# Graph attention on images: the output stores move from SyncE's DMA queue to ScalarE's, one slot later

## The reference, cut to what matters

```
alpha = relu(bn(wa @ x));  sigma = relu(bn(ws @ x))          # 32 x 2048 each
att   = softmax(mask8(alpha.T @ sigma))                       # each pixel sees its 8 neighbours
h_s   = x @ att.T
catt  = softmax(mask_pm1(x @ x.T))                            # each channel sees its two neighbours
h_p   = catt @ x
out   = (1 - gama) * x + gama * elu(h_s + h_p)
```

## Time and profile before

| | |
|---|---|
| Time, median of 3 runs | 399.77 us (397.32 to 403.58) |
| Profiled execution | 396.9 us, of which its span is 395.1 us |
| Busy PE, DVE, ACT, POOL | 355.2, 315.1, 306.2, 291.6 us |
| Granted TensorE clock, mean | 0.972 |
| DMA queue of SP | 136.76 MB |
| DMA queue of ACT | 0.07 MB |

### The profile page before, as it was taken

How to read it: one execution, slowest core, us unless ns; L and a number is a source line. 1 busy time by engine, 2 the same in 40 slices (tenths; PEclk the granted TensorE clock), 3 DMA queues, 4 the chain that set the end, 5 groups by cost and what they waited for, 6 DMA issues and landing times.

```text
span 395.1 us, 14345 instructions
## 1 busy us (share of the span) xinstructions
PE 355.2 (90%) x5487; PEld 270.0 (68%) x5488; DVE 315.1 (80%) x1072; ACT 306.2 (77%) x900; POOL 291.6 (74%) x198
## 2 busy tenths in 40 slices
PE   4869999999999999998999999899999999999663
PEld 1437868676786868677686768678676868768553
DVE  1065978889798878979897887979888897988894
ACT  3166788897878798887879788787878888787881
POOL 2103788878887888788778977887888778878980
PEclk8779999999999999999999999999999999999995
DMA  7999999999999999999999999999999999995124
GB/s 243 413 362 395 371 372 375 363 383 359 398 384 375 381 365 365 372 393 374 371 410 374 380 347 402 368 395 372 376 394 360 387 358 396 360 316 210 74 92 159
DMA packets 40613, 137.74 MB, mean 349 GB/s; under 512 B 3296, under 2 KB 3552, under 8 KB 36448
## 3 DMA queue, kind: packets, MB, share of 16 engines
q1 hardware_dynamic: 40256, 136.76, 92.8%
q10 hardware_dynamic: 288, 0.07, 0.1%
HBM read 103.26 MB, written 33.55 MB: 346 GB/s over the span
## 4 chain that ended last, share of the span: by engine, by line
PE 53%; DVE 23%; ACT 12%; issue 8%; DMA 2%; SPq 0%; DVEq 0%; ACTq 0%
PE z L468 22%; PE gb L468 21%; PE tr L543 7%; ACT score L281 7%; DVE probs L374 6%; DVE elu L389 5%; ACT z L301 3%; DVE z L383 3%; PE score L468 3%; DMA x<-x_dram 2%; DVE gb L404 2%; DVE band L400 1%; DVE row_inv L370 1%; ACT elu L308 1%; ACT probs_t L292 1%
## 5 line engine op out<-in xcount | busy, mean ns | idle before, releaser
L468 PEld LDWEIGHTS z<-probs_t,upper 64*128 64x128 f32 x2304 | 153.6, 189 | 44.6 <-issue 29.7
L468 PE MATMUL z<-probs_t,upper 64*128 64x128 f32 (+1 forms) x2304 | 171.3, 282 | 4.7 <-ACT probs_t L292 2.1
L247 POOL TENSOR_TENSOR blend<-elu,blend 128x1024 f32<-128x1024 f32 x62 | 146.2, 2358 | 9.5 <-POOL elu L243 0.4
L243 POOL TENSOR_SCALAR elu<-elu,vec,mix 128x1024 f32<-128x1024 f32 x62 | 74.0, 1193 | 76.4 <-DVE elu L389 76.3
L389 DVE SCALAR_TENSOR_TENSOR elu<-elu,z 128x512 f32<-128x512 f32 x124 | 79.5, 683 | 27.5 <-ACT elu L308 27.0
L308 ACT ACTIVATE elu<-z 128x512 f32<-128x512 f32 x128 | 69.7, 597 | 39.4 <-PE z L468 39.4
L301 ACT ACTIVATE z<-x,catt 128x512 f32<-128x512 f32 x128 | 83.6, 693 | 14.1 <-DVE catt L421 13.9
L383 DVE SCALAR_TENSOR_TENSOR z<-near,catt,z 128x512 f32<-128x512 f32 x128 | 90.4, 753 | 1.5 <-ACT z L301 1.5
L281 ACT ACTIVATE score<-score,neg_max 128x128 f32<-128x128 f32 x256 | 86.2, 337 | 6.2 <-DVE neg_max L365 6.2
L237 POOL TENSOR_SCALAR blend<-x,mix 128x1024 f32<-128x1024 f32 x64 | 72.0, 1125 | 7.4 <-DMA x<-x_dram 7.4
L468 PE MATMUL gb<-x,wt 128*32 128x256 f32 (+2 forms) x720 | 65.9, 484 | 2.1 <-DMA x<-x_dram 2.1
(11 more groups left out here) (49 smaller groups left out, 142.7 us busy)
## 6 DMA issues: line engine op xcount, KB each, us to landing
x<-x_dram SPq DMA_DIRECT2D x32, 1024.0 KB, 8.4
near<-x_near_dram SPq DMA_DIRECT2D x64, 512.0 KB, 7.7
out_dram<-blend SPq DMA_DIRECT2D x62, 512.0 KB, 7.0
upper<-x_t_dram SPq DMA_DIRECT2D x16, 1152.0 KB, 8.9
upper<-x_t_dram SPq DMA_DIRECT2D x16, 1024.0 KB, 9.0
out_dram<-blend SPq DMA_DIRECT2D x4, 256.0 KB, 2.0
const<-constants_dram SPq DMA_DIRECT2D x1, 291.5 KB, 12.8
const<-constants_dram SPq DMA_DIRECT2D x1, 128.0 KB, 2.2
```

Source lines behind the costliest of these rows:

```text
L243: nc.gpsimd.tensor_scalar(elu[s % 2][:, :, :], elu[s % 2][:, :, :], vec[:, V_GAMA:V_GAMA + 1], mix[:, 1:2], ALU.mult, ALU.add).then_inc(ga ...
L247: nc.gpsimd.tensor_tensor(blend[s % BLENDS][:, :, :], elu[s % 2][:, :, :], blend[s % BLENDS][:, :, :], ALU.add).then_inc(blend_done, 1)
L468: return nc.tensor.matmul(o, l, r, start=start, stop=stop, skip_group_check=True, **kw)
```

## The change

SP no longer stores. ACT does, on its own queue: at the beginning of slot t it waits for the blend of step t-3 and asks for its store, before `move_odd`, `move_even` and `exp_z` of that slot. Step 63 is stored after the loop. The waits, sizes and semaphores of each store stay as they were.

```diff
@@ SP's program
-            def store(s):
-                b, q = s // QUARTERS, s % QUARTERS
-                if s < TAIL:
-                    sp.wait_ge(blend_done, s + 1)
-                    sp.dma_start(out_img[b, :, :, q * QN:(q + 1) * QN], blend[s % BLENDS][:, :, :])\
-                        .then_inc(stored[s % BLENDS], 16)
...
                 if b + 1 < B:
                     load_near(b + 1, q)
-                if real(t - 2):
-                    store(t - 2)
@@ ACT's program
+            def store(s):
+                b, q = s // QUARTERS, s % QUARTERS
+                if s < TAIL:
+                    act.wait_ge(blend_done, s + 1)
+                    act.dma_start(out_img[b, :, :, q * QN:(q + 1) * QN], blend[s % BLENDS][:, :, :])\
+                        .then_inc(stored[s % BLENDS], 16)
+                else:
+                    for h in range(HALF):
+                        act.wait_ge(tail_done, 2 * (s - TAIL) + h + 1)
+                        act.dma_start(out_img[b, :, h, q * QN:(q + 1) * QN], blend[s % BLENDS][:, h, :])\
+                            .then_inc(stored[s % BLENDS], 16)
...
             for t in range(STEPS + 2):
                 b, q = t // QUARTERS, t % QUARTERS
                 ahead = b + 1 < B
+                if real(t - 3):
+                    store(t - 3)
                 if q == 1 and ahead:
                     move_odd(b + 1)
...
                 if q == 1 and ahead:
                     move_query(b + 1)
+            store(STEPS - 1)
```

## The result

The changed kernel takes 463.68 us in the median of 4 runs (460.32 to 466.3), the kernel before 398.54; the ratio is 1.169, with a 95% interval of 1.163 to 1.175. The profiled execution took 466.3 us, its span is 464.5.

The account below looks back on a forecast made before the run. PE was taken to bound the kernel before. 62 turns of 6.40 us plus moves of 6.3 and 7.7 give 410.8 against 349.6: +61.2 on a span of 395.1, 456.3; with run allowances 459 us, range 453 to 469.

Parts of the forecast that it names:

- the sum: From `exp_z` of step 0 to that of step 62: 62 turns plus the moves, 410.8 us against 349.6 before.
- The wait at the head closes a loop through POOL.: `exp_z`, DVE's elu, two POOL operations, ACT's store, next `exp_z`: one turn per slot, 5.75 us up to the issue.
- The issue costs 0.57 + 0.08 us.: On ACT after the wait: 0.57 us issue plus 0.08 to the next activation, making a plain turn 6.40 us.
- The first rival: On ACT: the issue doesn't hold ACT, only the wait does; a turn of 5.83, 424 us; chance 0.10 with cases between.
- The moves cost 0.45 and 0.51.: On ACT between store and `exp_z`: `move_odd` adds 0.45 us in 14 slots, `move_even` 0.51 in 15.
- The delay of DVE at q = 0 costs nothing.: DVE's elu, late behind the channel softmax in slots q = 0, costs nothing; at most 4.4 us.
- SP's relief and the landing cost nothing.: SP losing 62 + 4 store issues gains nothing; store landings, covered by two slots, cost nothing.
- "81% is more than that": PE, 81% busy after the change, keeps clock 1.00, since 68% busy between 375 and 385 had clock 1.00.
- The rival: Slower still: PE's gaps let the granted clock fall; over half of the images 34 us more, 493 us; chance 0.11.
- The DMA engines aren't a hidden bound.: Despite a DMA share of 1.02, DMA doesn't pace the kernel before: it has only 2% of the chain.
- What the profile after should show.: Turns 6.3 to 6.5 or about 6.9 us, ACTq rows 0.53 to 0.63, ACT idle over 1, DMA share near 0.87.
- A slot takes about 5.67 us because PE needs that.: In the kernel before, PE is busy 21.55 of 22.70 us per image, 95%, and so sets the slot's length.

Follow-up runs that it names:

- 1: Kernel before, with only ACT's wait for the blend of step t-3 added at the head of slot t, SP still storing: 418.65 us, ratio 1.055.
- 3: Changed kernel, but ACT stores step t-4 instead of t-3 in slot t: 400.37 us, ratio 1.005 to the kernel before.
- 4: Changed kernel, but ACT waits for and stores step t-3 in mid-slot after `move_probs`, not at the head: 399.48 us, ratio 1.003 to the kernel before.
- 5: Changed kernel, but POOL leaves out the multiplication by gama and the subtraction of gama: 397.00 us, ratio 0.999 to the kernel before.
- 2: Changed kernel, with ACT's wait kept at the slot's head but the store issued in mid-slot after `move_probs`: 420.89 us, ratio 1.058 to the kernel before.
- variant 7: Changed kernel, with `move_odd` and `move_even` put ahead of the store: 459.7 us, ratio 1.132 to the kernel before.
- 8: Changed kernel, with each transposition on PE made twice: 456.14 us, ratio 1.147 to the kernel before.
- the control: Kernel before, with each transposition on PE made twice: 414.93 us, ratio 1.036.

## Why the prediction was right, point by point

The forecast of 459 us lies 1% under the 464 measured, inside its own range of 453 to 469, and for the reason given. That the range held is luck in part: its upper end was made of a longer issue and of DVE's delay, neither of which came, and the clock's 10 us, which the sum didn't have, fell into the room they left.

- *The wait at the head closes a loop through POOL.* Shown from both ends: the wait alone costs 5.5% (1), moving the store out of the loop costs nothing (3, 4), and shortening POOL's part by 1.34 us returns all of the loss (5). The path from `exp_z` to the issue was put at 5.75 us and measures 5.75.
- *The issue costs 0.57 + 0.08 us.* It is 0.54 + 0.10, so a plain turn is 6.38 and not 6.40: two errors of 0.02 to 0.03 in opposite directions. That ACT stands still for its issue, taken from one row before a table load, holds only where the engine has nothing left in hand, as after a wait for the latest event. Elsewhere the issue runs beside the activations (2, 3, 4). The first rival, for which I gave 0.10, was wrong for the place and right for other places; with the price per issue taken as a constant, variants 3 and 4 would have been forecast too slow, and partly were.
- *The moves cost 0.45 and 0.51.* They cost 0.42 and 0.48, as the difference of the turns and as what variant 7 gave back.
- *The delay of DVE at q = 0 costs nothing.* Right: the turns from q = 0 are 6.80, which is 6.38 + 0.42.
- *SP's relief and the landing cost nothing.* Right; the chain still has 2% for DMA.
- *"81% is more than that", so the clock stays.* This step failed. The clock fell in five slots of the even move, 1.6 to 1.7 us each, 8.3 us, and in the last image, where one turn took 7.73 us instead of 6.38. That is the miss: `exp_z` of step 62 starts 452.00 - 32.28 = 419.7 us after that of step 0, and the sum had 410.8. With PE busier it goes (8). Three more turns of the last image took 6.5 to 6.7 us; they do so in variant 8 as well (6.67, 6.50, 6.74), and their 0.7 us have no cause shown. The row that I leaned on, 68% busy at full clock between 375 and 385, showed only that the clock can hold for so long, and the fall behind it stands in the same trace as the 3.88 us of the earlier trace rows. The factor of 1.43 taken from there was too low as well, since the clock fell in the middle of that group: it is 4.84 / 2.71 = 1.79. The rival had the right mechanism and far too large an extent.
- *The DMA engines aren't a hidden bound.* For the queue this is shown: in variants 3 and 4 the stores left the loads' queue at an unchanged pace, and nothing was gained. For the engines behind it only the control speaks, in which three slots of four grow with PE's work. The first agrees with the Trainium skill, DMA: Bandwidth & Descriptors, section "Issuing engines are not separate DMA queues", on the queue; what it says of the issuing engine holds in those variants and fails in the changed kernel by 65 us, because of the wait and of the issue that can't be hidden behind it.
- *What the profile after should show.* The turns and the ACTq rows came as told. ACT's idle time before the store was put at over 1 us; in the slots shown it is 1.28, 0.61 and 0.61 (the brackets less 0.64 or, before the move, 0.59). The DMA share was put at 0.87 and is 0.92, though GB/s fell from 383 to 317, and the clock didn't stay at 1.00.
- *"A slot takes about 5.67 us because PE needs that."* Too strong. In the control PE's extra 28 us cost 15: one slot of four hid its share whole, which a busy share of 95% didn't show.

## What to carry to other kernels

Before a DMA issue is moved to a compute engine, look up when that engine would come to the wait, and when the event comes: if the event is later, and if it descends from the engine's own last slot, the wait closes a loop, and where the loop is longer than the slot was, the slot becomes as long as the loop, however idle each engine is. One slot of distance, or a place in mid-slot, makes the same store free. And count an issue on such an engine only where the engine is out of work: it cost 0.64 us behind a wait and nothing behind queued activations.

## What was not expected of the hardware

- An engine made idler can cost time through PE's clock, and useless matmuls in PE's gaps won 8 us of 464 (granted clock 0.93 against 1.00 between 100 and 150 us).
- Two half stores issued in a row held ACT's sequencer for 0.82 to 1.77 us, 0.94 in the mean, one whole store of the same bytes for 0.54.
- At an unchanged pace of the kernel, a store on its own queue took longer to land than on the loads' queue: 10.2 us (variant 3) against 7.0, and 8.5 (variant 2) against the 6.4 of the wait alone. In the changed kernel, where the DMA engines have less to do in the time, it took 5.8.
